# Window attention of a two-layer kernel: three engines share the first tile's masked query copies, the first scores go ahead of the value projection, and the statistics of later tiles are spread over the first steps

## What is computed

```python
x = x + _L0_xattn_ref(_layernorm(x), ctx_4096, ...)   # window attention
x = x + _L0_ffn_ref(_layernorm(x), ...)               # gated FFN
x = x + _L1_xattn_ref(_layernorm(x), ctx_4096, ctx_4096, ...)
x = x + _L1_ffn_ref(_layernorm(x), ...)               # mixture of experts
```

```python
def _L0_xattn_ref(x, cond, Wq, bq, Wk, bk, Wv, bv, Wo, bo):   # B, C, T = 16, 64, 512
    q = _pointwise(Wq, bq, x); k = _pointwise(Wk, bk, cond); v = _pointwise(Wv, bv, cond)
    k, v = pad(k), pad(v)                     # 8 left, 7 right
    idx = jnp.arange(T)[:, None] + jnp.arange(16)[None, :]
    dots = jnp.einsum('bhdt,bhdtw->bhtw', qh, k_win) * scale     # 8 heads of 8 channels
    attn = jax.nn.softmax(dots, axis=-1)
    out = jnp.einsum('bhtw,bhdtw->bhdt', attn, v_win)
    return _pointwise(Wo, bo, out)
```

## Time and profile before

| | |
|---|---|
| median of 3 runs | 1142.29 us (1142.13 to 1146.94) |
| profiled execution, its own time | 1139.67 us |
| its span | 1137.8 us |
| TensorE, VectorE, ScalarE, GpSimd busy | 1032.8, 659.6, 387.9, 491.4 us |

### The profile page before, as it was taken

One profiled execution on the slowest core, in us unless ns is written; L12 is line 12 of the kernel. 1 busy time (PEld: TensorE's weight loads), 2 busy tenths in 40 slices (PEclk: granted clock), 3 DMA queues, 4 the chain that ended last, 5 costly groups with the idle time before them and its releaser, 6 DMA issues. The chain is left out here.

```text
span 1137.8 us, 23862 instructions
## 1 busy us (share of the span) xinstructions
PE 1032.8 (91%) x9074; PEld 850.9 (75%) x9074; DVE 659.6 (58%) x1380; ACT 387.9 (34%) x886; POOL 491.4 (43%) x547
## 2 busy tenths in 40 slices
PE   7888888999999879999999999999999999754994
PEld 3566667888887678888888888888888888533783
DVE  3887884544444675656555556656565565850324
ACT  3787864222222332222222222222322321511331
POOL 0544441332123345445454554444555542137645
PEclk7999999999999899999999999999999999985997
DMA  7000005574551021111011111111011100036768
GB/s 245 13 3 3 3 4 147 168 261 164 196 180 54 22 72 37 49 29 47 29 29 48 30 39 44 29 48 29 28 47 31 35 10 1 0 125 212 261 206 258
DMA packets 51802, 92.07 MB, mean 81 GB/s; under 512 B 10744, under 2 KB 24312, under 8 KB 51256
## 3 DMA queue, kind: packets, MB, share of 16 engines
q1 hardware_dynamic: 42104, 69.13, 19.1%
q10 hardware_dynamic: 6624, 12.06, 3.0%
q0 software_dynamic: 2976, 9.44, 2.6%
HBM read 77.25 MB, written 36.18 MB: 100 GB/s over the span
## 5 line engine op out<-in xcount | busy, mean ns | idle before, releaser
L121 PE MATMUL PS<-NTh,W 128*128 128x256 f32 (+2 forms) x688 | 216.5, 315 | 0.0
L122 PE MATMUL PS<-NTl,W 128*128 128x256 f32 (+2 forms) x688 | 214.0, 311 | 1.4 <-issue 1.4
L123 PE MATMUL PS<-NTh,W 128*128 128x256 f32 (+2 forms) x688 | 213.9, 311 | 0.0
L122 PEld LDWEIGHTS PS<-NTl,W 128*128 128x128 f32 (+1 forms) x688 | 131.0, 190 | 8.7 <-issue 1.8
L123 PEld LDWEIGHTS PS<-NTh,W 128*128 128x128 f32 (+1 forms) x688 | 129.1, 188 | 8.5
L121 PEld LDWEIGHTS PS<-NTh,W 128*128 128x128 f32 (+1 forms) x688 | 129.3, 188 | 7.3
L1448 POOL TENSOR_TENSOR W<-ca_raw,W 128x512 fp32r<-128x512 f32 x64 | 82.9, 1296 | 116.9 <-ACT W L1298 116.9
L1386 DVE TENSOR_REDUCE ca_su<-room 128x4 f32<-128x256 f32 x64 | 26.9, 420 | 156.0 <-ACT room L1314 156.0
L1415 DVE TENSOR_TENSOR room<-PS,ca_sinT 64x512 f32<-64x512 f32 (+1 forms) x192 | 115.0, 599 | 2.6
L121 PE MATMUL PS<-W,ca_aTh 128*128 128x512 f32 x256 | 106.3, 415 | 3.5 <-DVE X L1403 3.5
L1314 ACT ACTIVATE room<-room 128x256 f32<-128x256 f32 x64 | 26.9, 420 | 222.8 <-POOL room L1495 222.8
(11 more groups left out here) (241 smaller groups left out, 2332.9 us busy)
## 6 DMA issues: line engine op xcount, KB each, us to landing
ca_raw<-in_L_Wq SPq DMA_DIRECT2D x32, 256.0 KB, 2.8
ca_raw<-in_L_Wo SPq DMA_DIRECT2D x32, 256.0 KB, 2.7
rf_raw<-in_experts SPq DMA_DIRECT2D x28, 256.0 KB, 4.1
room<-slots ACTq DMA_DIRECT2D x23, 256.0 KB, 3.0
outs<-room ACTq DMA_DIRECT2D x23, 256.0 KB
outs<-blank SPq DMA_DIRECT2D x11, 512.0 KB, 9.2
room<-in_L_Wg SPq DMA_DIRECT2D x10, 256.0 KB, 2.8
room<-in_L_Wu SPq DMA_DIRECT2D x10, 256.0 KB, 3.0
```

The costliest lines, as they stand in the source:

```text
L121: nc.tensor.matmul(out, l_hi, r_hi, start=first, stop=False)
L122: nc.tensor.matmul(out, l_hi, r_lo, start=False, stop=False)
L123: return nc.tensor.matmul(out, l_lo, r_hi, start=False, stop=last)
```

## The change

Four things are altered, all inside `window_attention`.

- Tile 0's eight masked copies: ScalarE makes heads 0 to 2, VectorE heads 3 to 5, GpSimd heads 6 and 7. `q_ready` counts three sharers for tile 0 and one more for each later tile, made by ScalarE alone as before.
- TensorE: vproj of tile 0 and qproj of tile 1 move from ahead of the scores of unit 0 to behind them.
- VectorE: `xn` of tile 0 goes ahead of the `wo` products. The counts (BN_STATS) of tiles 2 to 7 are made in pairs at the end of steps 0, 1 and 2, aggregation and EPS at the end of step 2. The reciprocal and `xn` of tile 2 go to the end of step 3; `xn` of tile 2 stood at that step's beginning.
- ScalarE: the Sqrt for tiles 2 to 7 moves from step 0 to step 3, behind exp(2).

```diff
+    SHARERS = 3
@@ tensor
+                def project_rows(u, t):
+                    if t >= 0:
+                        pe.wait_ge(S["v_ready"], t + 1)
+                    if t >= 2:
+                        pe.wait_ge(norm.low_done, t - 1)
+                    pe.wait_ge(S["normed"], t + 2)
+                    nc.tensor.matmul(PJ, wT[:, 0, :], xn[:, (u // 4 + 1) % 2, :], start=True, stop=True).then_inc(S["q_mm"], 1)
...
+                        if q == 0 and n != 0:
+                            project_rows(u, t)
...
-                        if q == 2:
+                        if q == 2 and n != -2:
                             pe.wait_ge(S["k_ready"], t + 2)
                             project_context(t + 1, 2, S["v_mm"])
...
-                        pe.wait_ge(S["q_ready"], t + 1)
+                        pe.wait_ge(S["q_ready"], t + SHARERS)
...
                         last.then_inc(S["sc_mm"], 1)
+                    if n == 0:
+                        project_context(0, 2, S["v_mm"])
+                        project_rows(u, t)
@@ vector
                 normalise(0, 0)
+                for h in range(HH):
+                    last = nc.vector.tensor_scalar(wo[:, h, :], wT[:, 3, :], hh4[:, h:h + 1], None, ALU.mult)
+                last.then_inc(S["wo_ready"], 1)
+                vec.wait_ge(S["q_biased"], 1)
+                for h in range(3, 6):
+                    last = nc.vector.tensor_scalar(qx[:, 0, :, h, :], qp[:].rearrange("p (k t) -> p k t", t=BLK), hm[:, h:h + 1],
+                                                   None, ALU.mult)
+                last.then_inc(S["q_ready"], 1)
...
-                    if isinstance(n, int) and n == 0:
-                        statistics(2, range(FIRST, TT))
-
-                    if q == 3 and live(t + 2, TT) and (not isinstance(t, int) or t >= -1):
+                    if q == 3 and live(t + 2, TT) and t >= -1 and n != 3:
                         normalise(t + 2, slot)
...
+                    if n in range(3):
+                        later_counts((2 * n + 2, 2 * n + 3))
+                    if n == 2:
+                        later_variances()
+                    if n == 3:
+                        vec.wait_ge(S["std"], 2)
+                        nc.vector.reciprocal(rstd[:, FIRST:], std[:, FIRST:]).then_inc(S["rstd"], 1)
+                        vec.wait_ge(S["rstd"], 2)
+                        normalise(2, slot)
@@ gpsimd
+                gp.wait_ge(S["q_biased"], 1)
+                for h in range(6, WH):
+                    last = nc.gpsimd.tensor_scalar(qx[:, 0, :, h, :], qp[:].rearrange("p (k t) -> p k t", t=BLK), hm[:, h:h + 1],
+                                                   None, ALU.mult)
+                last.then_inc(S["q_ready"], 1)
@@ scalar
-                    if isinstance(n, int) and n == 0:
-                        deviations(2, range(FIRST, TT))
-
...
                         norm.root(act, t - 2, slot)
+                    if n == 3:
+                        deviations(2, range(FIRST, TT))
...
-                                act.wait_ge(S["q_ready"], 1)
+                                act.wait_ge(S["q_ready"], SHARERS)
...
-                    if q >= 1 and live(t + 1, TT):
+                    if q >= 1 and live(t + 1, TT) and (t >= 0 or q == 1):
```

More of the change, by code:

```diff
@@ L506, in _ @@
                 vec.wait_ge(S["w_ready"], 1)
-                for h in range(HH):
-                    last = nc.vector.tensor_scalar(wo[:, h, :], wT[:, 3, :], hh4[:, h:h + 1], None, ALU.mult)
-                last.then_inc(S["wo_ready"], 1)
                 def normalise(t, slot):
@@ L518, in _, with later_counts, later_variances @@
                 normalise(0, 0)
+                for h in range(HH):
[6 more added lines that the diff above has]
+                last.then_inc(S["q_ready"], 1)
+                def later_counts(tiles):
+                    for k in tiles:
+                        vec.wait_ge(x_loaded[k], 16)
+                        nc.vector.bn_stats(stats[:, k, :], sh.X[:, k, :]).then_inc(S["stats"], 1)
+                def later_variances():
+                    for k in range(FIRST, TT):
+                        vec.wait_ge(S["stats"], k + 1)
+                        nc.vector.bn_aggr(mv[:, k, :], stats[:, k, :]).then_inc(S["aggr"], 1)
+                    vec.wait_ge(S["aggr"], TT)
+                    nc.vector.tensor_scalar(veps[:, FIRST:], mv[:, FIRST:, 1], EPS, None, ALU.add).then_inc(S["veps"], 1)
                 def step(n, u, t):
                     q, slot = u % 4, u // 4
-                    if isinstance(n, int) and n == 0:
-                        statistics(2, range(FIRST, TT))
-                    if q == 3 and live(t + 2, TT) and (not isinstance(t, int) or t >= -1):
+                    if q == 3 and live(t + 2, TT) and t >= -1 and n != 3:
                         normalise(t + 2, slot)
@@ L664, in step @@
                                                         ACT.Copy, scale=hm[:, h:h + 1])
-                        if q == 3:
+                        if q == (3 if t >= 0 else 1):
                             last.then_inc(S["q_ready"], 1)
```

## The result

| | before | changed |
|---|---|---|
| median of 12 runs | 1140.83 us | 1150.84 us |
| ratio of the changed to before | | 1.0078, 95% interval 1.0065 to 1.0092 |
| profiled execution, span | 1137.8 us | 1153.6 us |

The change makes the kernel slower by 0.78% (8.9 us; the interval is 7.4 to 10.5). The forecast was +6.8 us on 1142.29; the range ended at 1151.5, which is +9.2. The profiled execution of the changed kernel was the slowest of its twelve (1155.76 us).

What follows compares the result with a forecast made beforehand. The start of tile 2's key projection was taken to decide the time: −4.87 + 6.28 (projections) + 0.38 + 1.44 (statistics) + 2.46 (`xn`) + 1.09 (load) = +6.8, 1149.1 us against the median 1142.29; range 1141.5 to 1151.5.

Steps and rivals of the forecast that it cites:

- rival D: GpSimd's copies of tile 0 take 3.0 us each, first scores 1.3 us later: 1150.4 us, chance 0.08.
- rival E: ScalarE's load back to Exp stops it for 1.28 us beyond the load's own row: 1150.4 us, chance 0.02.
- Gain 1: At the start, `xn` of tile 0 ahead of the `wo` products brings it forward by 0.79 us.
- gain 2: Tile 0's eight copies shared by three engines: first scores at 21.14 us instead of 26.01, −4.87 with the earlier `xn`.
- Loss 1: Projections and biases in series ahead of the second scores: VectorE's key(1) at 32.32 us against 30.91, +1.41.
- The clock up to 32 us: TensorE stays at half clock until the second scores are done, about 32 us.
- Rival A: TensorE's clock rises early, in the pauses around 25 us: 2.45 us less, +4.3, 1146.6 us, chance 0.22.
- Loss 2: Statistics inline on VectorE after key(1): key(2) at 35.75 us, +1.79, and key(3) at 40.46, +3.23.
- Loss 3: Tile 2's `xn` behind key(3), 1.24 us beside GpSimd's subtraction: scores of unit 4 at 44.39 us against 38.70, +5.69.
- Loss 4: Two more ScalarE table loads, the first hidden, the second 1.30 us: tile 2's key projection at 47.82 us against 41.04, +6.78.
- A shift there is a shift of the end: Later TensorE work stands behind tile 2's key projection, so its +6.78 us shift is passed on to the end.
- Rival C: Idle time in the steps after 41.04 us takes up the late start, nothing is left: 1142.3 us, chance 0.12.

Runs made afterwards that it cites:

- e1: The changed kernel with the statistics of tiles 2 to 7 back at step 0 and tile 2's `xn` back at the start of step 3; ratio to before 1.0019.
- e2: The kernel before with only the copies shared and `xn` of tile 0 ahead of `wo`, TensorE's order and statistics as before; ratio to before 0.999.
- e7: The changed kernel with all six counts and the variances at the start of step 0, Sqrt, reciprocal and tile 2's `xn` still late; ratio to before 1.0082.
- e5: The changed kernel with 7 identity products behind the scores of unit 2 and 20 behind those of unit 3, into an unread bank; ratio to before 1.0024.
- e6: The changed kernel with tile 2's `xn` made at the start of step 3 from tile 0's mean and deviation; ratio to before 1.0048.

## Why the prediction was right

The walk was right in its causes, and the time fell into the range with some luck. The range's end was +9.2 and the measured +8.9 has an interval up to +10.5; the largest chance, 0.51, was on a change within 0.5%. At kproj2 the +7.65 lies outside the forecast's own bounds, +5.6 to +7.3. By the time alone, rivals D and E at 1150.4 would fit no worse than the forecast's 1149.1; it is the rows that rule them out.

- Gain 1 and gain 2: right, −4.87 at scores(0). GpSimd's two copies took 3.80, the upper of the two bounds (4.2), and ended at 20.73, 0.8 ahead of ScalarE's; rival D, at 3.0 a copy, did not come.
- Loss 1, the series of projections: right, +1.40 at key(1); e1 and e2 show that the order alone turns a gain of 2.15 into a loss of 2.1.
- The clock up to 32 us: right; the window 14.00 to 31.00 has 0.50. Rival A fell.
- Loss 2, counts inline: key(2) and key(3) as forecast. That their cover was VectorE's idle time is shown by e1: with all statistics at step 0, key(0) comes 3.0 us later than in the changed kernel, key(1) at the same instant from the mark. Their share alone was not isolated (e7).
- Loss 3, the late `xn`, its collision: right in its start and in the 1.24. The step that was mis-sized is "43.39 + 1.0 = 44.39": I gave qproj2 full clock. It measured 1.84, and what follows ran at half clock too: 0.87 us in all, 1.16 by e5. The clock had fallen at about 37.6, after a pause of 1.70 ahead of scores(3) which my walk does not mention; e6, where `xn` comes early and the clock falls all the same, shows that the long wait for `xn` is not needed for it.
- Loss 4: the second load is on the path and lasts 1.29 from 46.56 to 47.85, no drain, so rival E falls and the trace again disagrees with the 2.66 us for a switch of the Trainium skill ("ScalarE: Activation LUTs", What ACT_TABLE_LOAD costs). Taking both loads away gave 0.7, since TensorE at half clock hides the rest. That the first load is hidden held only while `xn` was late anyway (e7).
- "A shift there is a shift of the end": in ten of the eleven experiments the two shifts agree within 0.3 us; the exception, e7, kept the half clock beyond kproj2. Rival C falls. The changed kernel's own profile adds 0.5 between them, of which 0.36 is a pause in TensorE's stream at 65 us ("issue") that I can't explain.

The sum was short by the clock's 0.9 at kproj2 and by this remainder; the time, +8.9 with an interval from 7.4, lies above +6.8 by somewhat more than that.

## What to carry to other kernels

Before an engine's work is put ahead of a wait, write down what stands behind it in program order: here 4.9 us won for the first unit were lost to the second, whose projections had been done under the copies. Work that costs nothing in one engine's idle time (six counts, a Sqrt while its table is in) costs its full length and more in a filled pipeline, and the first instruction that it delays decides. Where a change puts new waits into TensorE's stream, work the time out at both clocks, or keep it busy (here the fall came after a pause of 1.70 us, while in e2 one of 1.92 was passed at full clock, so the pause's length alone did not decide it): products into an unread bank gave 0.3% on the kernel before, 0.5% on sharing alone and 0.9% on the changed kernel by the ratios, a part of which lies outside the stage and is unexplained.

## What the runs showed of the hardware that I had not expected

- A GpSimd multiply of 128x512 by a column took 1.90 us, VectorE's 0.57, ScalarE's copy with a scale 0.65, for the same copies.
- TensorE's clock fell to 1.2 GHz between 37.00 and 38.00 us, only some 3 us after it had risen (PEclk 1.00 from 34.50 to 37.00), when TensorE had stood still from 35.36 to 37.06; kept busy in these waits, it stayed at 2.4 GHz in e5.
- `xn` on VectorE takes 0.55 us alone and 1.28 when it starts 0.06 behind a GpSimd operation of 1.05; when it starts first (35.31 before) it keeps its 0.54, and GpSimd's subtraction, from 35.48, took 1.28 instead of 1.05.
